# A two-block transformer kernel: the second block's token list by products of one-hot matrices instead of a table in memory, with barriers removed, weight loads cut in quarters, and ones multiplied while TensorE would wait

## What is computed

```python
x = x + L0_xattn(layernorm(x), ctx, bias)     # attention with an additive bias
x = x + L0_ffn(layernorm(x))                  # 32 experts, best 4 of a token, and a shared expert
x = x + L1_xattn(layernorm(x), ctx, mask)     # attention with a mask
x = x + L1_ffn(layernorm(x))                  # 8 experts, best 1 of a token:
# gate = x @ gate_w.T + b ; e = argmax(gate) ; h = relu(x @ w1[e] + b1[e]) ; out = h @ w2[e] + b2[e]
```

## Time and profile before

| | us |
|---|---|
| median of 3 runs (lowest, highest) | 855.77 (854.42, 856.27) |
| the profiled execution, its own time | 852.41 |
| its span in the profile | 850.5 |
| PE busy in the span | 733.1 (86%) |
| DVE busy | 444.8 (52%) |
| POOL busy | 323.6 (38%) |
| mean granted clock of PE, of full | 0.909 |

### The profile page before, as it was taken

The page is one execution under the profiler, slowest core; times in us unless marked ns, Lnnn a source line. Parts: engine busy times, 40 slices in busy tenths (PEclk is TensorE's granted clock), DMA queues, the critical chain, the costliest instruction groups (busy, mean ns, idle before and its releaser), DMA issues. The chain is left out here.

```text
span 850.5 us, 15538 instructions
## 1 busy us (share of the span) xinstructions
PE 733.1 (86%) x4441; PEld 606.9 (71%) x4442; DVE 444.8 (52%) x1628; ACT 322.1 (38%) x998; POOL 323.6 (38%) x348
## 2 busy tenths in 40 slices
PE   3899999899999999999937978888760499999995
PEld 2678888766666788888826757777650499999994
DVE  2678888546882633333337776788431133333331
ACT  1345545322222455555524665677520111222220
POOL 1234434100003555555437665534220334444421
PEclk8689999899999999999975896999855699999998
DMA  6522432420002555556932244426563465556540
GB/s 197 168 87 92 139 117 89 155 75 19 20 7 55 148 162 161 163 162 149 133 115 83 75 137 136 131 100 76 74 93 79 149 225 186 177 188 194 171 160 2
DMA packets 59940, 103.14 MB, mean 121 GB/s; under 512 B 20119, under 2 KB 41332, under 8 KB 58471
## 3 DMA queue, kind: packets, MB, share of 16 engines
q1 hardware_dynamic: 48070, 73.00, 29.6%
q0 software_dynamic: 11520, 27.24, 13.1%
q10 hardware_dynamic: 288, 2.10, 0.7%
HBM read 82.90 MB, written 22.15 MB: 124 GB/s over the span
## 5 line engine op out<-in xcount | busy, mean ns | idle before, releaser
L607 POOL DMA_INDIRECT U<-normed,idx_all x95 | 90.3, 950 | 159.6 <-DVE idx_all L1489 92.2
L1088 PE MATMUL bank<-R,U 128*128 x380 | 98.2, 381 | 0.0
L1143 PE MATMUL bank<-X,R 128*128 128x128 f32 x736 | 87.6, 278 | 0.0
L1143 PEld LDWEIGHTS bank<-X,R 128*128 128x128 f32 x736 | 85.8, 195 | 0.1
L1156 PE MATMUL bank<-R,X 128*128 x368 | 83.1, 379 | 0.0
L580 POOL DMA_INDIRECT R<-expert_out,slot x64 | 61.9, 967 | 34.5 <-issue 17.4
L1156 PEld LDWEIGHTS bank<-R,X 128*128 128x128 f32 x368 | 68.2, 190 | 8.4
L1580 DVE TENSOR_TENSOR U<-U,bank 128x128 f32<-128x128 f32 x95 | 27.3, 287 | 84.0 <-issue 78.4
L1088 PEld LDWEIGHTS bank<-R,U 128*128 128x128 f32 x380 | 64.8, 190 | 5.3
L592 POOL TENSOR_TENSOR U<-U,mx 128x1232 f32<-128x1232 f32 x16 | 36.0, 2248 | 79.2 <-DVE mx L1261 79.2
L708 ACT ACTIVATE U<-U,mx 128x77 f32<-128x77 f32 x256 | 65.5, 352 | 0.0
(11 more groups left out here) (194 smaller groups left out, 1535.8 us busy)
## 6 DMA issues: line engine op xcount, KB each, us to landing
R<-in_w SPq DMA_DIRECT2D x31, 1024.0 KB
R<-in_gu SPq DMA_DIRECT2D x8, 1024.0 KB, 5.4
expert_out<-U SPq DMA_DIRECT2D x48, 128.0 KB
expert_out<-xr SPq DMA_DIRECT2D x47, 128.0 KB
normed<-xr SPq DMA_DIRECT2D x32, 128.0 KB
R<-in_down SPq DMA_DIRECT2D x8, 512.0 KB, 4.0
x<-X SPq DMA_DIRECT2D x16, 128.0 KB
X<-in_x ACTq DMA_DIRECT2D x1, 1536.0 KB, 10.0
```

The costliest lines, as they stand in the source:

```text
L607: pool.indirect_dma_start(xg0[i % NXG], None, xn_d[0], bass.IndirectOffsetOnAxis(idx_all[:, i:i + 1], 0)).then_inc(EX[0]["gath"][i % NXG], 16)
L1088: mm = pe.matmul(bank[2 + u][:, 0:2 * F0], xgT0[u][:, c, :], gu_w[:, c, bass.ds(e, 1), :].rearrange("p a n -> p (a n)"), start=(c == 0), s ...
L1143: mm = pe.matmul(bank[1 + 2 * v + f // 4][:, (f % 4) * P:(f % 4 + 1) * P], w1_of[v][:, c, f * P:(f + 1) * P], xgT1[v][:, c, :], start=(c = ...
```

## The change

**The list.** The table in memory is gone: its filling at the start, the 16 scatters, the gather of its rows, and the transposes. In its place a matrix `list1` of 128 x 128 is built in a bank of PE's result memory. It has the token number at (slot // 128, slot % 128), plus one so that an empty place reads 0. For each tile a, DVE makes three one-hot matrices of 128 x 128 in bf16 (`one_hots1`), and PE multiplies them in two products that add to `list1` (`list_tokens1`). `split1` takes slot apart into its two halves. `plan1` makes the experts of the tiles directly as a row, and a selection matrix `pick1`; one product `list1 x pick1` picks the rows of the 24 tiles as columns (`pick_rows1`), and `rows1` turns empty places into numbers out of bounds and writes `idx_all`.

**Barriers.** Barriers 2 and 3 are gone. POOL waits for the saved tiles and for `idx_all`; SP, PE and DVE wait for `plan_e`. The gathers take their numbers from `idx_all` directly; `column` and its buffers are gone. The rows are gathered four tiles ahead instead of five.

**Loads.** SP's loop over the tiles of block 2 is written out. b2 is loaded in eight parts behind tiles 0 and 1, and the second matrices behind tiles 2 to 9, each in four parts of 256 KB (2 KB per partition). The second to fourth part of each wait for PE's q_mm, pv_mm and ot_mm of a later step.

**Ones.** `keep_busy(n)` multiplies the ones matrix n times with 512 columns of ones; nothing reads the result. It is called with 23 before PE's first wait and with 24 behind the first keys, with 6 in step -1 of block 1's attention, with 18 ahead of block 2's attention once tile 0's rows are gathered and with 14 in its step -1, with 4 in each of its steps 15 and 16, and with 14 ahead of the experts.

```diff
+            def keep_busy(n, b=7):
+                for _ in range(n):
+                    pe.matmul(bank[b][:, :], ones16[:, :], ones16[:, 0:1].to_broadcast([P, 512]), start=True, stop=True)
...
-            phase_barrier(pool, 2)
-            routing1(pool)
-            phase_barrier(pool, 3)
+            for u in range(2):
+                pool.wait_ge(RT["saved"][u], 16 * NT)
+            pool.wait_ge(R1S["x_saved"], 16 * NT)
+            pool.wait_ge(R0["idx_all"], 2)
...
+            for t in range(NT):
+                save_rows(sp, 1, t, t % 2)
+                save_x3(t)
+                if t < E1 + 2:
+                    for g in range(4):
+                        if g:
+                            sp.wait_ge(AT[(None, "q_mm", "pv_mm", "ot_mm")[g]], NT + t + (None, 5, 3, 3)[g])
+                        if t < 2:
+                            e = 4 * t + g
+                            sp.dma_start(b2_b[:, e], A["b2"][:, e].partition_broadcast(P)).then_inc(b12_in, 16)
+                        else:
+                            c = slice(g * FC1 // 4, (g + 1) * FC1 // 4)
+                            sp.dma_start(w2_w[:, t - 2, c], A["w2"][:, t - 2, c]).then_inc(w2_in, 16)
...
+                    if l == 1 and t >= NT - 2:
+                        done = (0, 12, 12, 14, 15, 16)[t - NT + 2:t - NT + 4]
+                        if done[1] > done[0]:
+                            split1(done[0], done[1], 4 * (0, 0, 1, 2, 3)[t - NT + 2])
+                        for a in (range(0, 4), range(4, 8), range(8, 14), (14,), (15,))[t - NT + 2]:
+                            one_hots1(a)
...
+            def list_tokens1(a):
+                pe.wait_ge(R0["one_hot"], NT + a + 1)
+                for g in range(2):
+                    mm = pe.matmul(bank[5][:, 0:P], oh_hi1[a % NOH][:, g, :], oh_lo1[a % NOH],
+                                   start=(a == 0 and g == 0), stop=(a == NT - 1 and g == 1), skip_group_check=True)
+                mm.then_inc(R0["placed_mm"], 1)
...
+            def one_hots1(a):
+                if a >= NOH:
+                    dve.wait_ge(R0["placed_mm"], NT + a - NOH + 1)
+                dve.tensor_scalar(oh_hi1[a % NOH][:, 0, :], iota16[:, :], hi_f[:, a:a + 1], tok_1,
+                                  ALU.is_equal, ALU.mult)
+                dve.tensor_scalar(oh_hi1[a % NOH][:, 1, :], iota16[:, :], hi_f[:, a:a + 1], float(P * a),
+                                  ALU.is_equal, ALU.mult)
+                dve.tensor_scalar(oh_lo1[a % NOH], iota16[:, :], lo_f[:, a:a + 1], None,
+                                  ALU.is_equal).then_inc(R0["one_hot"], 1)
```

More of the change, by code:

```diff
@@ L506, in save_x3 @@
                              x[:, bass.ds(t, 1), :].rearrange("p a n -> p (a n)")).then_inc(RTL[1]["x_saved"], 16)
[L508 to L519, removed]
+            for t in range(NT):
[11 more added lines that the diff above has]
+                            sp.dma_start(w2_w[:, t - 2, c], A["w2"][:, t - 2, c]).then_inc(w2_in, 16)
+            sp.wait_ge(R0["plan_e"], 2)
             sp_experts = [sp.alloc_register(f"sp_expert{i}") for i in range(4)]
@@ L549, in attention @@
                 T, TL = AT, ATL[l]
[L551 to L556, removed]
                 def step(t):
@@ L623, in rows @@
[L623 to L631, removed]
-            def results(i, u, v):
-                wait_apart(pool, X1["y2"], i + 1)
-                pool.indirect_dma_start(A["out"], bass.IndirectOffsetOnAxis(idx_out[v][:, :], 0), y1[u], None,
-                                        bounds_check=last_row, oob_is_err=False).then_inc(X1["out"][v], 16)
@@ new lines, in rows, with residual, results @@
+            def rows(i):
+                need(pool, X1["xt_mm"], i - 3)
+                gather(xg1[i % 4], xn_d[1], i, X1["gath"][i % 4])
+            def residual(i):
+                need(pool, X1["y2"], i - 1)
+                gather(x3g[i % 2], x3_d, i, X1["gath3"][i % 2])
+            def results(i):
+                pool.wait_ge(X1["y2"], i + 1)
+                pool.indirect_dma_start(A["out"], bass.IndirectOffsetOnAxis(idx_all[:, i:i + 1], 0), y1[i % 2], None,
+                                        bounds_check=last_row, oob_is_err=False).then_inc(X1["out"][i % 4], 16)
@@ L934, in step @@
                         mm.then_inc(RT["xt_mm"], 1)
+                    if t == -1:
+                        keep_busy(14 if l else 6)
+                    if l == 1 and t >= NT - 1:
+                        for a in {NT - 1: range(0, 4), NT: range(4, 8), NT + 1: range(8, 14), NT + 2: (14,)}[t]:
+                            list_tokens1(a)
                     if l == 0 and t == NT - 1:
@@ new lines, in plan1, with rows1 @@
+                dve.wait_ge(plan, 5)
+                dve.tensor_scalar(pick1, tile_less, own_first1, None, ALU.is_equal).then_inc(R1S["pick"], 1)
+            def rows1():
+                listed = bank[7][:, P:P + PLAN1]
+                dve.wait_ge(R1S["picked"], 1)
+                dve.tensor_scalar(idx_tens[:, 0:PLAN1], listed, 0.0, float(SKIP), ALU.is_equal,
+                                  ALU.mult).then_inc(R1S["plan"], 1)
+                dve.wait_ge(R1S["plan"], 6)
+                dve.scalar_tensor_tensor(out=idx_all[:, 0:PLAN1], in0=listed, scalar=-1.0, in1=idx_tens[:, 0:PLAN1],
+                                         op0=ALU.add, op1=ALU.add).then_inc(R0["idx_all"], 1)
```

188 lines of the change are left out of this document (90 added, 98 removed).

## The result

The changed kernel takes **824.5 us**, median of 4 runs (823.42 to 824.68), against 856.02 us of the kernel before on the same chip (854.42 to 857.05, 4 runs): ratio 0.967, 95% interval 0.963 to 0.971. The profiled execution took 824.4 us with a span of 822.2, 28.3 us under the span before.

What follows compares the result with a forecast made beforehand. Bounds: full-clock expert work, POOL's 17 us drain and the chain behind it, a step 13 stall, half-clock stretches. 20.0 + 5.4 + 4.7 - 3.1 + 3.2 + 2.5 = 32.7 us off 855.8 gives 823 us; range 812 to 838.

Steps and rivals of the forecast that it cites:

- From the last slot to the experts: Last slot to the second expert tile's transposes: 32.65 us would become 12.7, saving 20.0 us, bounds 18 and 22.
- The rival of the drain: POOL's 17.1 us drain returns as a wait, first gather 17 us late: 840 us, chance 0.07.
- The stall: Step 13: DVE would no longer wait for its program behind scatters and a load, gaining 5.4 us, bounds 0 and 5.4.
- The start: Ones at the kernel's start hold full clock, halving DVE's waits for first scores and values: 3.2 us gained.
- The start of block 2's attention: The 18 ones ahead of it halve DVE's 4.47 us wait for the first values: 2.5 us gained.
- The last steps: Steps 14 to 16 of block 2's attention at full clock: 4.7 us gained, upper bound 8.8, lower bound 0.
- DVE's new work: One-hot matrices and splits in steps 14 to 17: 3.1 us lost on the path, bounds 1 and 5.
- no DRAIN between the attention and the experts: Sign: the changed profile would show no DRAIN on POOL between block 2's attention and the experts.
- the first gather: Sign behind the last slot: the prediction is wrong if this stands more than 6 us behind it.
- DVE waited over 3 us ahead of the values: Sign: DVE would have no idle time over 3 us ahead of its reads of the values in any step.
- the output projection: Sign: its four products would take 1.1 us in steps 14 to 16.
- DVE had gaps: Sign: DVE would be busy without a gap from its last normed tile in step 15 to `idx_all`.

Runs made afterwards that it cites:

- c1: The changed kernel with the 16 scatters issued again into a table nobody reads, quarter loads, no barrier: 842.9 us, ratio 0.980 to the kernel before.
- b3: The changed kernel with second matrices loaded whole, 1 MB behind every second tile, no scatters: 825.7 us, ratio 0.963 to the kernel before.
- c4: The changed kernel with both the scatters and the whole 1 MB loads put back: 848.2 us, ratio 0.989 to the kernel before.
- the first pair: The kernel before and the changed kernel, first measured on one chip, not known which: 856.02 and 824.5 us, ratio 0.967.
- a2: The changed kernel with only the start's ones (23, 24 and 6) kept: 804.9 us, ratio 0.9704 to the kernel before.
- a1: The changed kernel without any product of ones: 808.0 us, ratio 0.9725 to the kernel before.
- the second chip: Chip on which the changed kernel and the kernel before were rerun unchanged, beside variants of loads and barrier; the kernel before took 854.4 us there.
- b4: The changed kernel with a barrier of all five engines put back behind block 2's attention, no scatters: 827.0 us, ratio 0.968 to the kernel before.
- group 1: Four variants of the changed kernel, on ones and the spread of one-hot matrices, run on a chip where the kernel before took 829.8 us.
- a4: The changed kernel with one-hot matrices dealt 6, 6, 2, 1, 1 over steps 14 to 18, not 4, 4, 6, 1, 1: 801.0 us, ratio 0.965.
- a3: The changed kernel without the 18 and 14 ones at the start of block 2's attention: 805.9 us, ratio 0.9704 to the kernel before.
- b1: The changed kernel run again unchanged, on another chip: 828.1 us, ratio 0.9694 to the kernel before.
- c3: The changed kernel with one-hot matrices dealt 6, 6, 2, 1, 1 and whole 1 MB loads, no scatters: 824.4 us, ratio 0.956 to the kernel before.
- b2: The kernel before, run again unchanged: 853.2 us, ratio 1.002 to itself.
- c2: The changed kernel with the scatters and the barrier behind block 2's attention put back: 844.7 us, ratio 0.985 to the kernel before.

## Why the prediction was right

The predicted 823 us is 1.5 us from the median. The profiled spans show 28.3 us of gain against a sum of 32.7; the medians show 31.5, since the profiled execution of the kernel before was 3.4 us under its median. By the terms of the sum:

- **From the last slot to the experts, 20.0.** Measured 19.6: 13.05 us in place of the predicted 12.7. `idx_all` was ready 4.3 us behind the slot (predicted 3.9), the first gather 0.9 behind it (1.0), the transposes 7.82 behind the gather (7.8). The reason that I gave why POOL's 17 us would not come back was thin ("the saved tiles can't hold POOL"). The runs show that the scatters make the DRAIN long, and that with them 7.2 us of it come back without any barrier (c1), as a wait for the saves and slower gathers. The rival of the drain would have been right in part, had the scatters stayed: the way is then longer by 7.2 us and not by 17. It didn't come about since they went with the table.
- **The stall, 5.4.** Measured 5.5. The reason was half right: I named the scatter and the load together. b3, c1 and c4 show that the scatters do it without a load of 1 MB, and that such a load does not do it.
- **The start, 3.2.** Measured 5.4 in the first pair; a2 against a1 gives 2.3 by the second values and 2.9 by the last DRAIN ahead of block 2. On the second chip the changed kernel reached that DRAIN at 434.2 and the kernel before at 433.6, so there the term was -0.6. The clock fell at 28.0 for 13.7 us there, and in the first execution of the same kernel at 27.9 for 3.4; but b3 and b4, with a fall of 3.4 us too, reached the DRAIN at 434.6 and 433.5, so the length of the fall is not the whole reason. The term's size is right only as a mean over values from -0.6 to 5.4. (By its own rule the first half was 1.7 and not 1.4: half of 3.44; and by the earlier trace rows 512 columns take 0.24 us and not 0.22, which moves no term.)
- **The start of block 2's attention, 2.5.** This step failed: measured -0.9. The 18 ones did raise the clock (full from 441.0), but ACT then waited 3.35 us with a remote releaser while PE stood still, and the clock was back at half from 447.8 to 458.0. On the chip of group 1, where ACT waited 1.25 us there, the term was 1.6 to 2.0 (a4 against a1 and a3). b1 lost 3.70 us in the same way, and c3 3.07 us at the same place with no remote releaser named, so the late ACT counts and not the name of the releaser. On the second chip the term was -1.6 (34.7 us from the DRAIN to the first values in b1, 33.1 in b2).
- **The last steps, 4.7 at full clock less 3.1 for DVE's new work.** Expected 1.6 of gain, measured 3.2 of loss. The step that failed is that ones would hold the clock there. In a3 and b4 they did for the most part, with 8 us at half behind step 13's values, and the stretch took 29.6 us, 1.9 less than before, near the predicted 1.6. In the changed kernel's two profiles 21 us were at half and it took 34.7 and 34.6. In a2, without ones there and 20.5 us at half, it took 32.5. So when the clock is down all the same, the ones cost some 2 us. What decides whether it stays up is not shown: the kernels with these ones had 8 to 12 us at half in a3, a4, b3, b4 and c3. DVE's six sets did come on the path (626.86, no idle time where the earlier trace rows has 2.26).
- **The middle steps**, which I left out, gave 2.6 in the first pair and -0.4 in the second (127.0 us in b2, 127.4 in b1, for twelve steps). In these steps every profile but those of group 1 shows waits with a remote releaser (7.6 us of them before, 8.5 in b2, 11.3 in b1, 14.6 in the changed kernel), and those of group 1 none (106.9 us for the same twelve steps in a2). How many there are changes from one execution to the next, and their sum does not order the times: the changed kernel has the most of the four and is the fastest of them, 120.7 us. The difference between executions here, up to 7 us, is larger than most terms of the sum.

That the total came out within 2 us is thus partly luck: 2.2 too little for the start and 2.6 not counted in the middle against 3.4 and 4.8 too much for the attention's start and the last steps, and then a profile before that was 3.4 us under its median.

Of the signs that the prediction named, these held: no DRAIN between the attention and the experts, 13.05 us from the last slot to the transposes, the first gather 5.2 us behind the slot (it allowed 6). These failed: DVE waited over 3 us ahead of the values of steps 0 and 15 (3.65 and 3.91), the output projection was at full clock only in step 14, DVE had gaps of 1.01, 1.40 and 0.76 us in step 16, and block 2's first scores ran at half clock.

Not shown: that a remote releaser means a wait for the engine's program. Instruction packets arrive near such waits (at 444.4 ahead of the one at 447.00), but they arrive elsewhere too. Why the chip of group 1 has none is open.

## What to carry to other kernels

A long DRAIN on the engine that issues indirect transfers is not a fixed price of the barrier: here it took 2.7 to 17.4 us. Before a barrier is removed, look at which indirect transfers that engine issued since its last DRAIN, and how lately, and take those away first. The 4-byte scatters here cost little in their own queue's row and much in the plain queue's, so look at the share of the DMA engines per megabyte of the plain queue. A gain that hangs on the granted clock should be priced as a range with zero in it (the start gave -0.6 to 5.4 us here), and read over several executions.

## What was not expected of the hardware

- The same kernel before took 829.8 us on one chip, 854.4 and 860.4 on two others and 856.0 in the first pair. Between a2 and b1, two forms of the changed kernel, 23 us lie between the medians, and the twelve middle steps of block 2's attention differ by 20.4 in the profiles.
- PE stayed at half clock for 17.10 us in which it was busy 16.86 (the fourth row of the first view of the result), so a busy PE alone did not bring the clock back there; it had fallen there with PE busy 8.15 of the 10 us around (594 to 604).
- With 200 packets of the scatters' queue beside it (c1), the plain queue needed 31% of 16 engines' time per megabyte, against 11% in b1 without them (59.2 / 1.88 and 25.4 / 2.21).
- POOL's DRAIN ran on for 11.3 us (c2) and 10.4 us (before) with no packet on any DMA queue, and the DRAIN at the end of the kernel was 1.3 us longer with scatters that had been issued 190 us earlier (c1, c4).
